# Routing the second experts in two parts, the first inside the attention, and masking transposed scores with one full-height matmul per head

## What is computed

```python
# attention: 16 heads of size 8, causal, with rotary positions
s = (q @ k.T) * 8 ** -0.5            # 512 x 512 for each head and batch
s = where(key <= query, s, -inf)
x = x + gate * (softmax(s) @ v) @ W_o.T
# mixture: 8 experts of 512 hidden columns
h = layernorm(x) * (1 + scale) + shift
logits = h @ Wr                       # 2048 x 8
vals, idx = top_k(logits, 2)
weight = softmax(vals)[0]             # of the best against the second best
y = gelu(h @ W1[idx[0]]) @ W2[idx[0]] # the best expert alone
x = x + gate * weight * y
```

## Time and profile before

| | us |
|---|---|
| median of 3 runs (579.58 to 580.09) | 580.0 |
| profiled execution | 577.07 |
| its span | 575.2 |
| TensorE busy in the span | 452.4 (79%) |
| VectorE busy | 392.0 (68%) |
| ScalarE busy | 278.1 (48%) |
| GpSimd busy | 271.6 (47%) |
| end of the last transposed scores' probabilities | 461.9 |
| first scatter into slots | 485.3 |
| first block's tokens on TensorE | 510.1 |
| last block's result copied | 558.5 |

### The profile page before, as it was taken

The page is one execution under the profiler, slowest core; times in us unless marked ns, Lnnn a source line. Parts: engine busy times, 40 slices in busy tenths (PEclk is TensorE's granted clock), DMA queues, the critical chain, the costliest instruction groups (busy, mean ns, idle before and its releaser), DMA issues.

```text
span 575.2 us, 10088 instructions
## 1 busy us (share of the span) xinstructions
PE 452.4 (79%) x3120; PEld 274.4 (48%) x3120; DVE 392.0 (68%) x1264; ACT 278.1 (48%) x518; POOL 271.6 (47%) x392
## 2 busy tenths in 40 slices
PE   3688778987998999994558998999999863059970
PEld 3545456766653444442323434435445343049970
DVE  5789738988655888886679687888898235025533
ACT  1568796653453544441223577678777831013220
POOL 4210038998301786664641047476655502714541
PEclk9988889999799999997775799999999985559995
DMA  8600000000335333310386012222300000141114
GB/s 354 169 1 1 0 2 2 1 2 1 144 148 125 99 106 99 107 62 2 108 208 124 4 31 88 82 86 85 84 5 4 3 0 10 52 123 36 36 38 146
DMA packets 25739, 39.94 MB, mean 69 GB/s; under 512 B 3228, under 2 KB 17756, under 8 KB 25164
## 3 DMA queue, kind: packets, MB, share of 16 engines
q1 hardware_dynamic: 21752, 30.42, 17.8%
q0 software_dynamic: 3936, 8.89, 5.2%
HBM read 27.55 MB, written 11.55 MB: 68 GB/s over the span
## 4 chain that ended last, share of the span: by engine, by line
PE 49%; DVE 18%; POOL 11%; issue 8%; ACT 6%; DMA 6%; SPq 0%; DVEq 0%; POOLq 0%; ACTq 0%
PE ps L1579 5%; PE ps L1581 5%; PE ps L1568 5%; PE ps L1686 4%; PE ps L1599 3%; PE ps L1771 3%; PE ps L1782 3%; POOL slots_x L586 3%; DVE rows L406 3%; PE ps L1391 2%; DVE moe L1221 2%; PE ps L1641 2%; POOL qk_parts L305 2%; DVE st L387 2%; PE ps L1672 2%
## 5 line engine op out<-in xcount | busy, mean ns | idle before, releaser
L1221 DVE CUSTOM_DVE_ANT_0 moe<-ps,const 128x512 bf16<-128x512 f32 (+3 forms) x256 | 110.5, 486 | 9.7 <-PE ps L1641 9.4
L778 ACT ACTIVATE arena<-ps 128x256 f32<-128x256 f32 (+3 forms) x128 | 85.8, 701 | 33.6 <-PE ps L1672 32.9
L476 POOL TENSOR_TENSOR arena<-arena 128x512 f32<-128x512 f32 x32 | 51.7, 1616 | 51.9 <-DVE arena L1139 51.7
L1641 PE MATMUL ps<-arena 48*128 48x128 bf16 (+3 forms) x256 | 56.1, 329 | 10.7 <-DVE arena L1221 4.7
L1672 PE MATMUL ps<-arena 51*128 51x128 bf16 (+3 forms) x256 | 52.2, 307 | 0.0
L1686 PE MATMUL ps<-arena 128*32 128x512 f32 (+3 forms) x512 | 48.4, 450 | 0.9 <-ACT arena L778 0.6
L1667 PE MATMUL ps<-bconst 64*128 64x64 bf16 x512 | 45.6, 195 | 1.2 <-ACT arena L778 0.5
L1641 PEld LDWEIGHTS ps<-arena 48*128 48x128 bf16 x256 | 16.7, 97 | 55.7 <-DVE arena L1221 31.7
L751 ACT ACTIVATE arena<-arena 128x512 f32<-128x512 f32 x32 | 20.2, 630 | 41.9 <-DVE arena L1139 41.6
L838 ACT ACTIVATE arena<-ps 128x512 f32<-128x512 f32 x23 | 13.7, 597 | 55.0 <-PE ps L1771 55.0
L592 POOL DMA_INDIRECT tokens_y<-arena,token_at x23 | 22.1, 960 | 32.5 <-DVE arena L1325 31.3
(11 more groups left out here) (239 smaller groups left out, 1113.2 us busy)
## 6 DMA issues: line engine op xcount, KB each, us to landing
arena<-expert_weights SPq DMA_DIRECT2D x32, 256.0 KB, 3.2
arena<-moe_in SPq DMA_DIRECT2D x1, 4100.0 KB, 12.8
qk_parts<-arena SPq DMA_DIRECT2D x24, 128.0 KB, 2.3
qk_parts<-arena POOLq DMA_DIRECT2D x24, 128.0 KB, 2.3
arena<-qk_parts POOLq DMA_DIRECT2D x32, 96.0 KB, 2.5
arena<-qk_parts SPq DMA_DIRECT2D x8, 288.0 KB, 5.6
moe<-moe_in SPq DMA_DIRECT2D x1, 1936.0 KB, 13.8
slots_x<-zeros SPq DMA_DIRECT2D x1, 1518.0 KB, 19.6
```

The costliest lines, as they stand in the source:

```text
L476: pool.tensor_tensor(yacc[:, ts], yacc[:, ts], pr[:, i % 2, :], ALU.add).then_inc(sem("yacc"), 1)
L778: act.activation(pt[:, u % 4, :, 0:n], ps[:, 4 + 2 * k:6 + 2 * k, 0:n], ACT.Exp, scale=ATT_SCALE).then_inc(sem("probs"), 1)
L1221: v.tensor_tensor_reduce(out=junk[:, done % 2, 0:n], in0=ps[:, k, col:col + n], in1=w["mask"][:, (3 - qt) * P:4 * P], scale=1.0, scalar=3 ...
L1641: mm = pe.matmul(ps[:, k, col:col + n], qaug[lo:lo + KR, b % 2, 2 * g + j // 2, qt * P:(qt + 1) * P], kaug[lo:lo + KR, b % 2, 2 * g + j // ...
```

## The change

- **Mask.** The constant `causal` becomes one 128 x 128 matrix, and `scores_T` issues one matmul per head of 128 rows and 128 columns against `identb`: two for a unit where there were four.
- **Two parts.** The router's work is done for batches 0 and 1 and for batches 2 and 3 apart (`PARTS = 2`, `PT = 8` token tiles each), with 15 blocks each, 30 in all. Slots, counters and index arrays exist for each part.
- **The first part's routing goes into the attention loop**: `h4_T` of batches 0 and 1 at (11, 6) and (12, 1), `logits` at (12, 4), `ranks` at (13, 4) on TensorE as items of the ring (`ROUTER_AT`); `choose`, `expert_blocks`, `positions`, `block_experts`, `second_best` and `top_weight` on VectorE at (12, 5) to (14, 2); the exponential of the second-best weight on ScalarE at (13, 7). GpSimd makes the router input earlier and sends the first part's eight scatters directly after its loop.
- **The blocks of the first part follow the loop at once**, and between them stand the last step's output, the router input of batch 3 and the routing of the second part. GpSimd returns eight blocks of the first part, scatters the second part, returns the rest, and adds batches 0, 1 and 2; VectorE adds batch 3. Block results are written over the block's tokens (`xb`), not to `ys`.
- The loops end at iteration 15; what iteration 16 did stands after them. Loads of constants share a semaphore.

The diff, cut to its core:

```diff
+PARTS = 2
+PT = NT // PARTS
+NBLK = PT + E1 - 1
...
+        ROUTER_AT = {(11, 6): ("h4T", 0), (12, 1): ("h4T", 1), (12, 4): ("logits", 0), (13, 4): ("ranks", 0)}
```

SyncE, slot loads:

```diff
+            slots = slots_x.rearrange("(a j p) d -> a p j d", p=P, a=PARTS)
+            for a in range(PARTS):
+                sp.wait_ge(sem(f"scattered{a}"), 16 * PT)
+                if a == 0:
+                    sp.wait_ge(sem("pv"), 4 * QG * (B - 1))
+                for c, js in enumerate(BLOCK_GROUPS):
+                    sp.dma_start(xb[a][:, js, :], slots[a, :, js, :]).then_inc(sem(f"ld_slots{a}{c}"), 16)
```

GpSimd, after its loop:

```diff
+            to_slots(0)
             router_input(2, 1)
             router_input(2, 2)
             ln_rstd(pool, 4, B - 1)
+            for j in range(RETURNED_FIRST):
+                to_tokens(0, j)
+            to_slots(1)
+            for j in range(RETURNED_FIRST, NBLK):
+                to_tokens(0, j)
             for j in range(NBLK):
+                to_tokens(1, j)
+                if j in (4, 7):
...
+                    combine(pool, b, "y_weighted0", "x4_pool", b + 1)
             pool.wait_ge(sem("gate_weights"), NT)
+            combine(pool, 2, "y_weighted0", "x4_pool", 3)
```

ScalarE, in and after its loop:

```diff
+                    if (it, i) in ((11, 7), (12, 2)):
+                        h4_T(it - 11)
+                    if (it, i) == (13, 7):
+                        top_exp(0)
+
+            weighted(NT - 1)
+            h4_T(2)
+            gelu(0)
+            attention_T(B - 1)
+            for n in range(1, 6):
+                gelu(n)
+            h4_T(3)
+            for n in range(6, PARTS * NBLK):
+                gelu(n)
+            top_exp(1)
```

VectorE, in and after its loop:

```diff
+                    if (it, i) == (12, 5):
+                        choose(0)
+                    elif (it, i) == (13, 5):
+                        expert_blocks(0)
+                    elif (it, i) == (13, 6):
+                        positions(0)
+                    elif (it, i) == (13, 7):
+                        block_experts(0)
+                        second_best(0)
+                    elif (it, i) == (14, 2):
+                        top_weight(0)
...
+            weights_in(0)
+            block_in(0)
+            o_norm(NT - 1)
+            weights_in(1)
+            block_in(1)
+            block_tokens(0)
+            weights_in(2)
+            block_in(2)
+            attn_out(B - 1)
+            router_input(B - 1, 0)
+            router_input(B - 1, 1)
+            block_out(0)
+            router_input(B - 1, 2)
+            router_input(B - 1, 3)
+            block_step(2)
+            router_input(B - 1, 4)
+            block_step(3)
+            for i in range(4, 7):
+                gate_weights(2 * (i - 4))
+                gate_weights(2 * (i - 4) + 1)
+                block_step(i)
+            choose(1)
+            block_step(7)
+            expert_blocks(1)
+            block_step(8)
+            positions(1)
+            block_step(9)
+            block_experts(1)
+            second_best(1)
```

TensorE, the masks, and after its loop:

```diff
-                for qh in range(2):
-                    for hh in range(2):
-                        bank, lo = 4 + 2 * (u % 2) + hh, HALF * hh
-                        pe.matmul(ps[:, bank, HALF * qh:HALF * (qh + 1)],
-                                  w["causal"][lo:lo + HALF, qh * P:(qh + 1) * P], w["half"][lo:lo + HALF, :],
-                                  start=(qh == 0), stop=True, skip_group_check=True)
+                for hh in range(2):
+                    pe.matmul(ps[:, 4 + 2 * (u % 2) + hh, 0:P], w["causal"], identb, start=True, stop=True,
+                              skip_group_check=True)
...
+            weighted_values(4 * NT - 1)
             pe.wait_ge(sem("probs"), 128)
+            ring_free(pe, 2, RING_MAIN)
+            block_in(0)
+            o_T(NT - 1)
+            h4_T(2)
+            block_in(1)
+            block_hidden(0)
+            a_T(B - 1)
+            block_step(1)
+            attn_out(B - 1)
+            for i in range(2, 6):
+                block_step(i)
+            h4_T(3)
+            block_step(6)
+            logits(1)
+            block_step(7)
+            ranks(1)
+            for i in range(8, NBLK):
+                block_step(i)
```

535 lines of the change are left out of this document (311 added, 224 removed).

## The result

Over four runs each the changed kernel has a median of 632.6 us (625.4 to 641.7), the kernel before 579.8 (577.2 to 580.1), and the ratio is **1.084, 95% interval 1.075 to 1.093**. The profiled execution took 625.4 us with a span of 623.4 (before 577.07 and 575.2, which is 1.9 us apart and not 2.1), so it is 48.2 us longer than the span of before. Forecast were 589 (570 to 602): right in sign, far outside the range.

What follows compares the result with a forecast made beforehand. The prediction took TensorE, busy 94% in the attention, and a serial tail of 113.2 us as the bounds. Masks +23, routing +7 and tail -21 gave +9 on the median of 580.0: 589 us, range 570 to 602.

Steps and rivals of the forecast that it cites:

- The masks: Attention: full-height masks cost shape switches, streams and lost overlap of the halves, partly hidden by waits; +23 us (+12 to +33).
- T: The start of the attention's last value matmuls, 462 in the earlier trace, from which the prediction counts the tail's times.
- the 4 us for a weight load of its own: Masks: the first full-height matmul's weights can't be loaded ahead after a switch; 0.04 us a unit over 104 units.
- near zero: Attention: expected sign of the masks' cost, TensorE's waits on VectorE near zero in iterations 1 to 12.
- Rival (a): Attention: existing waits cover most of the masks' new holes; masks +10, routing +3, tail -25, 568 us; chance 0.25.
- The routing inside the attention: Iterations 11 to 14: routing of batches 0 and 1 adds work on TensorE, VectorE and ScalarE; +7 us (+3 to +10).
- Nothing on it is due until the last two iterations are over: GpSimd in the attention: its first-part scatters of 10.1 us delay nothing that is needed soon, so no cost.
- sixteen logits: Routing on TensorE: these matmuls take about 1.9 us at full clock, 2.1 with switches.
- VectorE's 1.3 us for being ahead of the maxima: Iteration 13: 18 routing steps stand before maxima for which TensorE's ring waits, costing about 1.3 us.
- ScalarE's 1 to 3 us before the small exponential: Iteration 13: expected sign, ScalarE waits for VectorE's last routing step; priced at 1.6 us for TensorE.
- The tail: From the last value matmuls to the end: blocks start at once, end at T+92.5 against T+113.2; -21 us (-27 to -9).
- VectorE's last two pairs of operations: Return at the end: these go, 0.69 us each operation, 2.8 us, helping shorten the return from 16.7 to 14 us.

Runs made afterwards that it cites:

- run 2: The kernel before with the full-height masks alone; 605.4 us, ratio 1.044 (1.036 to 1.051).
- Run 3: The kernel before with each half-height mask matmul issued twice, as many added columns without a change of shape; 584.2 us, ratio 1.008.
- run 5: The changed kernel with the old half-height masks, GpSimd's router inputs put back where they stood and the routing following later; 595.4 us.
- run 7: The changed kernel as it is, executed and traced once more; 627.4 us.
- runs 8 and 15: The changed kernel with its second scatter burst behind all first-part returns, 644.8 us; the changed kernel with both scatter bursts broken in two, 627.2 us.
- run 12: The changed kernel with old masks and moved GpSimd and ScalarE steps, plus the first scatter burst held until the attention's last values; 597.2 us, one execution.
- run 9: The changed kernel with old masks, GpSimd's router inputs as before, ScalarE's evacuations ahead of the probabilities and the small exponential later; 587.8 us.
- run 13: The changed kernel with old masks, moved steps and split scatter bursts, plus the first half's routing behind the attention's last maxima; 585.8 us.
- run 14: The changed kernel with old masks, moved steps, split bursts and late routing, plus two waited-for clearings inside the second scatter burst; 586.2 us.
- run 1: The changed kernel with the half-height masks of before; 587.9 us, ratio 1.015 (1.007 to 1.024) against the kernel before.
- run 10: The changed kernel with old masks and moved GpSimd and ScalarE steps, plus VectorE's third block step ahead of two router steps in the tail; 589.5 us.

## Why the prediction was right or wrong

**The masks, right.** Forecast +23 (+12 to +33), alone +26.6, +25.1 from iteration 0 to T by the traces. Each of the 256 full-height masks was seen, a full iteration takes 9.97 us where 9.7 was said, and TensorE changes shape 27 times in it instead of 11. Two small misses nearly cancel: the waits absorbed less than said (below), and the 4 us for a weight load of its own aren't there, since the first mask starts 0.09 us behind the scores' stream, like any change of shape. The two masks of a unit start 0.066 us apart, where the prediction had 0.056 for a stream: 1 us over 104 units. The groups of iterations 0 to 15 by form, where the earlier trace rows has 222 ns for 128 columns of 51 rows:

```profile
L1829 PE MATMUL ps<-bconst 128*128 128x128 bf16 x256 | 38.8, 237 | 5.7 <-ACT arena L836 5.2 <-DMA arena<-arena 0.6
L1833 PE MATMUL ps<-arena 51*128 51x128 bf16 x64 | 7.5, 232 | 0.0
```

and the waits from 325.6 to 458 us:

```profile
PEld ps L1805 <- DVE arena L1302: 12.5, 21, 0.8
...
PE ps L1805 <- DVE arena L1302: 1.1, 5, 0.2
```

Weight loads still wait 12.5 us for the ring where the earlier trace rows has 21.9 (12.6 over twelve iterations in the masks-only kernel), so that some 9 us were absorbed, not 12, and "near zero" was wrong for them; the matmuls' own waits did fall, from 3.0 to 1.1. Rival (a), waits that cover the masks, fell with run 2. The rule on a change of tiling mode that the prediction took from the Trainium skill (TensorEngine Tiling (Array Packing), Key Properties) holds here, with 0.09 to 0.10 us for each change. Run 3 puts the changes, with the lost overlap, at 21 of the 26.6 us.

**The routing inside the attention, wrong: +25.7, not +7.** The list of what is added on TensorE and VectorE was complete; the failing steps are one sentence on GpSimd's queue, an omission on ScalarE's, and the clock.

"Nothing on it is due until the last two iterations are over", "so no cost", said of GpSimd, was wrong twice. I looked only at the stores. The change moves a router input of 4.6 us from iteration 10 to 8, ahead of the maxima's parts: 5.8 us in run 5, with the old masks. With the longer iterations of the new masks a wait of about 1 us is left, and the three iterations 9 to 11 lose 3.5 us beside the masks-only kernel in the first trace, 7.8 in run 7's and 17.7 in those of runs 8 and 15, where the half clock follows the wait; no run separates the two. And the stores themselves, which end where nothing waits for them, come with late signals of TensorE: without them iterations 14 and 15 to T are 8.2 us shorter (run 12).

ScalarE's evacuations of the transposes weren't costed at all. In the changed kernel they stand behind a slot's probabilities and hold one of three ring banks:

```profile
457.64 0.37 PE L1805 MATMUL ps<-arena 48*128 48x512 bf16 x1 [0.92 <-ACT hT L873]
...
462.96 0.39 PE L1805 MATMUL ps<-arena 48*128 48x384 bf16 x2 [1.32 <-ACT hT L873]
466.04 3.58 PE L1893 MATMUL ps<-arena,hT 128*128 128x8 f32 x16
```

The third row is the term of the sum that was mis-sized by the clock: sixteen logits in 3.58 us, not 1.9. They and most of the rest of iteration 12 (458.2 to 479.3) run at the 1.2 GHz level, granted from 464.5 to 478.2; this iteration alone has 9.5 of the 25.7 us. I had priced the attention at full clock because all of the earlier trace rows's stretch has it; the changed order didn't keep it. In run 9 the sixteen take 1.85 us at full clock, as forecast, and iteration 12 takes 12.0 us. Which of run 5's moves keeps the clock up isn't settled. VectorE's 1.3 us for being ahead of the maxima are 3.4 by run 13, ScalarE's 1 to 3 us before the small exponential 3.05.

With these causes moved away the attention pays 7.3 us from iteration 9 to T (run 14), the size that I had forecast, and the tail then waits 6.2 for the slots. The forecast priced an ideal placement, not the one written down. Naming for each moved step what is queued behind it on its engine would have found GpSimd's router input and ScalarE's evacuations; the late signals no row of before could show.

**The tail, wrong: -6.5, not -21.** Its marks in T, forecast, run 1 and the changed kernel: block 14 out at 45, 47.3, 56.9; last block out at 77.5, 82.3, 89.1; end at 92.5, 100.0, 106.7. So 7.5 us are missing without any late signal: 2 from the later start of part two, 2.8 in its fifteen blocks, 2.7 in the return. (The forecast's own terms, 77.5, 1.5 and 14, add up to 93.0 and not to 92.5.) The return's step failed like this: I took VectorE's last two pairs of operations off the end, but GpSimd's load, multiplication and addition of its own half end as late:

```profile
606.61 0.96 POOL L633 DMA_INDIRECT tokens_y<-arena,token_at  x1 [0.30 <-issue]
608.86 0.93 SPq L404 DMA_DIRECT2D arena<-tokens_y  x2
611.86 1.26 POOL L444 TENSOR_TENSOR arena<-arena 128x512 f32<-128x512 f32 x1 [4.28 <-DMA arena<-tokens_y]
...
613.19 1.59 POOL L446 TENSOR_TENSOR x<-x,arena 128x512 f32<-128x512 f32 x1
...
615.36 0.82 SPq L412 DMA_DIRECT2D y_out<-x  x2
```

From the last store to the landing of the output this is one chain, 17.6 us from the last block's copy to the end as against 17.0 before. The other 9.6 us are the late signals; the second part makes up 2.8 of them, since its slots are there when it starts (run 1 waits 1.79 us for them) and its clock is full. Right were the gap of 4.33 us up to T+14.8 (3 to 5 at T+10 to 14) with its cause (run 10), the positions at T+34.4 (32), and the second part's wait for its slots, 1.79 us in run 1 (2).

**The start.** Iteration 0 starts 4.0 us later. In the other traces, whose programs hardly differ up to there, it starts between 0.4 and 6.6 us later than in the trace of before (the changed kernel's second: 2.7). The forecast had nothing for it, and no run explains it.

**The range.** It was worked out from the terms' own bounds, and every bound of the routing supposed that TensorE would meet no new gap. With gaps, late signals and the half clock all terms could only grow. Its upper end, 602, isn't even the sum of the terms' own upper ends, which is 614 (+33, +10 and -9); the measured time is above that too.

## What to carry to other kernels

Before a step is moved on an engine that isn't the bound, write down what is queued behind it and when the bound engine needs that: 4.6 us on GpSimd, 57% busy in the earlier trace rows, cost 5.8 us on TensorE. A matmul of full array height between half-height ones costs a switch on either side and the overlap of the halves, so that fewer instructions can be slower: two matmuls for four cost 27 us over 128 units. And when a reverted part gives back far more than it costs alone, look for a third thing which differs between the two traces before adding the numbers up.
